# The last product of a gated feed-forward layer: one f32 product per block becomes three float32r products of exactly split operands

## The reference, cut to what matters

```python
def act_qdq(x):                      # 16 bit: one scale over the whole tensor
    qmax = 2.0 ** 15 - 1.0
    scale = jnp.maximum(jnp.max(jnp.abs(x)) / qmax, 1e-12)
    return jnp.clip(jnp.round(x / scale), -qmax - 1.0, qmax) * scale

x = act_qdq(x)
up = act_qdq(x @ lpbq_dequant(w_up).T)        # (8, 512, 768)
gate = act_qdq(x @ lpbq_dequant(w_gate).T)
sig = fixed_qdq_u16(jax.nn.sigmoid(gate))
gate = act_qdq(gate * sig)
o = act_qdq(gate * up)                        # (8, 512, 768)
return o @ lpbq_dequant(w_down).T             # (8, 512, 256), added to x
```

## Time and profile before

| | |
|---|---|
| median of 3 runs | 1388.59 us (1387.4 to 1388.69) |
| span of the profiled execution, first to last instruction | 1382.0 us |
| TensorE (PE) busy | 1284.0 us, 93% |
| VectorE (DVE) busy | 977.2 us, 71% |
| ScalarE (ACT) busy | 839.3 us, 61% |
| GpSimd (POOL) busy | 502.6 us, 36% |
| last block, first product to last | 1295.57 to 1378.6 us |

### The profile page before, as it was taken

How to read it: one execution, slowest core, us unless ns; L and a number is a source line. 1 busy time by engine, 2 the same in 40 slices (tenths; PEclk the granted TensorE clock), 3 DMA queues, 4 the chain that set the end, 5 groups by cost and what they waited for, 6 DMA issues and landing times. The chain is left out here.

```text
span 1382.0 us, 21094 instructions
## 1 busy us (share of the span) xinstructions
PE 1284.0 (93%) x7272; PEld 635.7 (46%) x7272; DVE 977.2 (71%) x1703; ACT 839.3 (61%) x1453; POOL 502.6 (36%) x670
## 2 busy tenths in 40 slices
PE   9999799999999999999999999999998999950799
PEld 5566323334343343434545554555444444420587
DVE  5876598887878878786666788887743435987522
ACT  4455337776777767777565556556553437959432
POOL 4455200235344454434673433333330003639200
PEclk9999869999999999999999999999999999975899
DMA  8999674233424243342343643333110001316132
GB/s 288 376 339 325 230 176 111 82 87 93 124 68 127 78 122 105 93 124 75 99 133 94 197 121 101 93 99 109 33 32 16 1 0 73 155 70 250 57 95 91
DMA packets 88190, 170.74 MB, mean 124 GB/s; under 512 B 14867, under 2 KB 49431, under 8 KB 86551
## 3 DMA queue, kind: packets, MB, share of 16 engines
q1 hardware_dynamic: 87547, 168.16, 39.2%
q10 hardware_dynamic: 539, 1.26, 0.4%
HBM read 108.26 MB, written 60.31 MB: 122 GB/s over the span
## 5 line engine op out<-in xcount | busy, mean ns | idle before, releaser
L1329 DVE TENSOR_REDUCE b_neg_max<-b_score 128x1 f32<-128x512 f32 (+3 forms) x864 | 541.2, 663 | 177.6 <-PE b_score L877 93.5
L1102 ACT ACTIVATE b_probs<-b_exp 128x512 f32<-128x512 f32 (+1 forms) x864 | 463.3, 581 | 281.9 <-PE b_exp L901 281.0
L874 PE MATMUL b_score<-b_k_stack,b_q_stack 97*128 97x512 bf16 (+3 forms) x1024 | 356.2, 351 | 14.7 <-issue 8.8
L901 PE MATMUL b_exp<-b_q_stack,b_k_stack 100*128 100x512 bf16 (+3 forms) x1024 | 344.6, 342 | 6.4 <-ACT b_probs L1102 5.6
L922 PE MATMUL b_av<-b_probs,b_values 128*17 128x512 f32 (+3 forms) x2048 | 228.5, 518 | 3.7 <-POOL b_probs L1200 3.4
L874 PEld LDWEIGHTS b_score<-b_k_stack,b_q_stack 97*128 97x128 bf16 x1024 | 99.8, 98 | 250.7 <-DVE b_neg_max L1329 128.5
L901 PEld LDWEIGHTS b_exp<-b_q_stack,b_k_stack 100*128 100x128 bf16 x1024 | 100.1, 98 | 82.6 <-ACT b_probs L1102 24.9
L1200 POOL TENSOR_SCALAR_AFFINE_SELECT b_probs<-b_probs 128x512 f32<-128x512 f32 x96 | 61.7, 643 | 176.7 <-ACT b_probs L1102 176.2
L1208 POOL CAST b_max_parts<-b_neg_max 128x16 bf16<-128x16 f32 x64 | 12.9, 202 | 286.3 <-DVE b_neg_max L1329 284.1
L877 PE MATMUL b_score<-diag_qk,minus_big 128*128 128x128 bf16 x512 | 112.6, 220 | 0.0
L1756 POOL TENSOR_TENSOR f_hidden<-f_tmp,f_hidden 128x2048 int32<-128x2048 int32 x8 | 44.3, 5532 | 137.7 <-DVE f_tmp L1708 137.7
(11 more groups left out here) (212 smaller groups left out, 1821.4 us busy)
## 6 DMA issues: line engine op xcount, KB each, us to landing
b_q_stack<-s_q SPq DMA_DIRECT2D x384, 64.0 KB
s_k<-a_part_k SPq DMA_DIRECT2D x48, 256.0 KB, 3.3
b_k_stack<-s_k SPq DMA_DIRECT2D x61, 192.0 KB
s_up<-f_up SPq DMA_DIRECT2D x6, 1536.0 KB, 5.0
s_va<-a_va SPq DMA_DIRECT2D x16, 544.0 KB, 5.4
b_values<-s_va SPq DMA_DIRECT2D x16, 544.0 KB, 4.1
a_mask_q<-mask_in SPq DMA_DIRECT2D x8, 1024.0 KB, 8.2
b_k_stack<-s_k SPq DMA_DIRECT2D x61, 128.0 KB
```

Source lines behind the costliest of these rows:

```text
L874: mm = pe.matmul(o, q, KS[half][0:R_MAX, h, 0:w], start=True, stop=causal or not general)
L901: mm = pe.matmul(o, k, QS[half][0:NSTACK, h, q0:T], start=True, stop=not masked)
L1102: nc.scalar.activation(probs[kc][:, h0:h0 + m, q0:T], exp_bank[n % RINGS][:, 0:m * w].rearrange("p (h n) -> p h n", h=m), ACT.Exp).then_in ...
L1329: nc.vector.tensor_reduce(neg_max[u][:, qt, h0:h0 + m], score_bank[n % RINGS][:, 0:m * w].rearrange("p (h n) -> p h n", h=m), AX.X, ALU.ma ...
```

## The change

The product of an f32 tile with f32 weights is replaced by three products in float32r (F32R below), a 4-byte type that keeps fewer bits of the mantissa and that TensorE takes in one pass. `w_downT` is split once into `down_high` (its value rounded to float32r) and `down_low` (what is left, written over `w_downT`). The activation is kept as the rounded integer, without its scale, and split in the same way into `o_high` and `o_low`. TensorE adds low x high, high x low and high x high into the same PSUM bank, 18 products for each row tile where there were 6, and the scale is applied in the last addition.

- POOL makes `down_high` (a copy) and `down_low` (a subtraction), each 128x1536, at the head of its stream in the first block; DVE gets a `memset` of `minus_magic` at the head of its stream there.
- ScalarE: after the two shifts of a half it also makes `o_high` (128x1536, bias -MAGIC), but for batch 0.
- DVE: `unshift` goes; `low` makes `o_low` = (od - MAGIC) - o_high, 128x1536, from two SBUF tiles; for the four pieces of batch 0 it also makes `o_high`. `add` becomes a `scalar_tensor_tensor` (PSUM times scale plus x). The order is low(b, u), add(b-1, u).
- TensorE: 576 products for 192; it waits for `lows`, and for `down_split` once.
- The loops of the third block are unrolled on every engine.
- `o_high` lies in the room of the two `up` tiles, `o_low` in that of `normed`'s batches 2 and on.

```diff
+                    nc.vector.memset(minus_magic[:, :], -MAGIC)
                     nc.vector.memset(sig_unit[:, :], 2.0 ** -16).then_inc(unit_set, 1)
...
+                    nc.gpsimd.tensor_copy(down_high[:, :, :], w_downT[:, :, :]).then_inc(down_split, 1)
+                    pool.wait_ge(down_split, 1)
+                    nc.gpsimd.tensor_tensor(down_low[:, :, :], w_downT[:, :, :], down_high[:, :, :].bitcast(F32), ALU.subtract).then_inc(down_split, 1)
                     for b in range(NB):
                         gates(b)
...
+                    def round_off(b, u):
+                        here = part_of(b, u)
+                        if b > 1 and u == 0:
+                            act.wait_ge(lows, piece(b - 2, pieces(b - 2) - 1))
+                        shift(od[b % 2][:, 0:MINE, here], at(b)[:, 0:MINE, here], "prod")
+                        shift(od[b % 2][:, MINE:FC, here], whole(b)[:, MINE:FC, here], "prod").then_inc(shifted, 1)
+
+                    def high(b, u):
+                        here = part_of(b, u)
+                        act.wait_ge(shifted, piece(b, u))
+                        if b > 1:
+                            act.wait_ge(full, 2 * (b - 2) + u + 1)
+                        nc.scalar.activation(o_high[b % 2][:, :, here], od[b % 2][:, :, here], ACT.Identity, bias=minus_magic[:, 0:1]).then_inc(highs, 1)
+
+                    for b in range(NB):
+                        for u in range(pieces(b)):
+                            round_off(b, u)
+                            if b > 0:
+                                high(b, u)
...
                                 t = 2 * u + j
-                                if pieces(b) == TT:
-                                    pe.wait_ge(dequant, t + 1)
-                                for f in range(FC):
-                                    mm = pe.matmul(down[2 * half + u][:, j, :], od[half][:, f, t * P:(t + 1) * P], w_downT[:, f, :], start=(f == 0), stop=(f == FC - 1))
+                                if b == 0:
+                                    pe.wait_ge(lows, piece(0, t))
+                                terms = [(o, wt, f) for o, wt in ((o_low, down_high), (o_high, down_low), (o_high, down_high)) for f in range(FC)]
+                                for n, (o, wt, f) in enumerate(terms):
+                                    mm = pe.matmul(down[2 * half + u][:, j, :], o[half][:, f, t * P:(t + 1) * P], wt[:, f, :], start=(n == 0), stop=(n == len(terms) - 1))
                             mm.then_inc(full, 1)
...
-                            unshift(od[half][:, :, here], od[half][:, :, here], "prod").then_inc(dequant, 1)
+                    def low(b, u):
+                        here = part_of(b, u)
+                        if b == 0:
+                            dve.wait_ge(shifted, u + 1)
+                            nc.vector.tensor_scalar(o_high[0][:, :, here], od[0][:, :, here], -MAGIC, None, ALU.add).then_inc(first_highs, 1)
+                            dve.wait_ge(first_highs, u + 1)
+                        else:
+                            dve.wait_ge(highs, 2 * (b - 1) + u + 1)
+                        if b > 1:
+                            dve.wait_ge(full, 2 * (b - 2) + u + 1)
+                        nc.vector.scalar_tensor_tensor(out=o_low[b % 2][:, :, here], in0=od[b % 2][:, :, here], scalar=-MAGIC,
+                                                       in1=o_high[b % 2][:, :, here].bitcast(F32), op0=ALU.add, op1=ALU.subtract).then_inc(lows, 1)
...
-                            nc.vector.tensor_tensor(x, down[2 * half + u][:, :, :], x, ALU.add).then_inc(added, 1)
+                        nc.vector.scalar_tensor_tensor(out=x, in0=down[2 * half + u][:, :, :], scalar=scales["prod"][0][:, 0:1], in1=x,
+                                                       op0=ALU.mult, op1=ALU.add).then_inc(added, 1)
```

More of the change, by code:

```diff
@@ L9 @@
 F32 = mybir.dt.float32
+F32R = mybir.dt.float32r
 BF16 = mybir.dt.bfloat16
@@ L1470, in gated_ffn_phase @@
         hidden = sb("hidden", [P, FC, NB, T], F32)
+        down_high, down_low = sb("down_high", [P, FC, D], F32R), weights.down_low
+        o_high = [nc.alloc_sbuf_tensor_at(f"f_o_high{i}", [P, FC, T], F32R, offset=nc.sbuf_base + 4 * FC * T * i) for i in range(2)]
+        o_low = [nc.alloc_sbuf_tensor_at(f"f_o_low{i}", [P, FC, T], F32R, offset=const["normed_at"] + 4 * (2 * TT * D + FC * T * i)) for i in range(2)]
+        down_split = sem("down_split")
         up = [sb(f"up{i}", [P, FC, T], F32) for i in range(2)]
@@ L1478, in gated_ffn_phase @@
         units = {"act": sig_unit, "prod": sb("unit_prod", [P, 1], F32)}
+        minus_magic = sb("minus_magic", [P, 1], F32)
+        first_highs = sem("first_highs")
         unit_set = sem("unit_set")
@@ L1834, in gated_ffn_phase, with piece, part_of @@
             x_stored = [sem(f"x_stored{i}") for i in range(2)]
-            shifted, dequant, full, added = (sem(f"down_{n}") for n in ("shifted", "dequant", "full", "added"))
-            EXTRA = TT - 2
+            shifted, highs, lows, full, added = (sem(f"down_{n}") for n in ("shifted", "highs", "lows", "full", "added"))
             def pieces(b):
-                return TT if known(b) and b == 0 else 2
+                return TT if b == 0 else 2
+            def piece(b, u):
+                return u + 1 if b == 0 else TT + 2 * (b - 1) + u + 1
+            def part_of(b, u):
+                n = T // pieces(b)
+                return slice(u * n, (u + 1) * n)
             with nc.Block() as block:
@@ L1847, in rows @@
                         return dram["out"][b].rearrange("(t p) d -> p t d", p=P)
-                    def step(b, half, k):
-                        if not known(b):
-                            wait_apart(sp, x_stored[half], 16 * k)
+                    for b in range(NB):
+                        half = b % 2
+                        if b > 1:
+                            sp.wait_ge(x_stored[half], 16 * (b // 2))
                         sp.dma_start(XL[half], rows(b)).then_inc(x_landed[half], 16)
-                        if not (known(b) and b == 0):
-                            wait_apart(sp, added, 2 * b)
+                        if b > 0:
+                            sp.wait_ge(added, 2 * b)
                             sp.dma_start(rows(b - 1), XL[1 - half]).then_inc(x_stored[1 - half], 16)
-                    over_batches(sp, step)
                     for u in range(2):
@@ L1865, in _ @@
                 def _(act):
[L1866 to L1875, removed]
+                    def round_off(b, u):
[10 more added lines that the diff above has]
+                        nc.scalar.activation(o_high[b % 2][:, :, here], od[b % 2][:, :, here], ACT.Identity, bias=minus_magic[:, 0:1]).then_inc(highs, 1)
+                    for b in range(NB):
+                        for u in range(pieces(b)):
+                            round_off(b, u)
+                            if b > 0:
+                                high(b, u)
                 @block.tensor
                 def _(pe):
-                    def step(b, half, k):
+                    keep_busy(pe, const, over[1], 11)
+                    pe.wait_ge(down_split, 2)
+                    for b in range(NB):
+                        half = b % 2
                         for u in range(2):
-                            if pieces(b) == 2:
-                                pe.wait_ge(dequant, 2 * b + u + 1 + EXTRA)
-                            if not known(b):
+                            if b > 0:
+                                pe.wait_ge(lows, piece(b, u))
+                            if b > 1:
                                 pe.wait_ge(added, 2 * (b - 2) + u + 1)
@@ L1891, in step @@
+                                for n, (o, wt, f) in enumerate(terms):
+                                    mm = pe.matmul(down[2 * half + u][:, j, :], o[half][:, f, t * P:(t + 1) * P], wt[:, f, :], start=(n == 0), stop=(n == len(terms) - 1))
                             mm.then_inc(full, 1)
-                    keep_busy(pe, const, over[1], 11)
-                    over_batches(pe, step)
                 @block.vector
                 def _(dve):
[L1898 to L1902, removed]
-                            unshift(od[half][:, :, here], od[half][:, :, here], "prod").then_inc(dequant, 1)
@@ L1917, in _ @@
-                    over_batches(dve, step)
-                    add(NB - 1, 1, NB // 2 - 1)
+                    def low(b, u):
[6 more added lines that the diff above has]
+                            dve.wait_ge(highs, 2 * (b - 1) + u + 1)
+                        if b > 1:
+                            dve.wait_ge(full, 2 * (b - 2) + u + 1)
+                        nc.vector.scalar_tensor_tensor(out=o_low[b % 2][:, :, here], in0=od[b % 2][:, :, here], scalar=-MAGIC,
+                                                       in1=o_high[b % 2][:, :, here].bitcast(F32), op0=ALU.add, op1=ALU.subtract).then_inc(lows, 1)
@@ new lines, in add @@
```

(16 more changed lines are left out.)

1 line of the change is left out of this document (added).

## The result

| | before | changed |
|---|---|---|
| median of the runs | 1387.99 us (1383.9 to 1388.69, 4 runs) | 1376.91 us (1372.42 to 1378.31, 4 runs) |
| ratio | | 0.9918, 95% interval 0.9897 to 0.9939 |
| span of the profiled execution | 1382.0 us | 1376.6 us |

The change made the kernel 11.1 us faster (interval about 8.5 to 14.3). The forecast was a saving of 17.2 us, to 1371.4 us; the measured time lies inside the stated range of 1368.8 to 1378.5, 5.5 us above that value.

What follows compares the result with a forecast made beforehand. TensorE's products were taken to bound the third block (busy 83.11 of 83.20 us). Against the span of 1382.0: -20.1 +1.06 +0.05 +1.7 +0.06 = -17.2, so 1364.8, plus 6.6 around it 1371.4 us; range 1368.8 to 1378.5.

Steps and rivals of the forecast that it cites:

- third rival: Third block: another engine or a half-hidden load sets the pace; 1374 to 1384 us, chance 0.13.
- One pass in place of four: Third block, TensorE: 576 float32r products of one pass replace 384 instructions of f32 products; 20.1 us saved.
- rival of 0.216 us a product: Third block: a float32r product streams like every other 4-byte operand, at 0.216 us; 1433 us, chance 0.10.
- The size of the product's term: Third block: products 0.109 us apart, 62.95 us in all where 83.04 stood; 20.1 us saved.
- bf16 row: Profile row of four bf16 products of the same 256 columns, 0.110 us each, used as a lower bound for float32r's price.
- The load: Third block, TensorE: loads of the stationary tile near 140 ns, of which about 57 ns grows with the columns.
- That a load hides at all: Third block: loads hide under products in flight; the rival, an exposed load, gave 0.166 us a product, 1404 us, chance 0.03.
- DVE behind POOL: Head of first block: DVE's first unshift waits for POOL's subtraction, gates 1.7 us later; rival of no hold-up 1369.6, chance 0.12.
- The first product: Start of third block: DVE's high, a wait and low replace unshift, so the first product starts 1.06 us later.
- ScalarE, DVE and the transfers hidden: Third block, per batch: ScalarE 7.2 us and DVE 5.1 under TensorE's 7.85; transfers 7.2 against 11.8 us.
- margin of 0.3 us a half: Third block: ScalarE's spare time under TensorE's products in each half of a batch, 0.3 us.
- low end: Lower limit of the stated range: no stall at the head, 1369.6, and products 108 ns apart, 1368.8 us.

Runs made afterwards that it cites:

- bf16 run: The changed kernel with GpSimd's split of the weights moved later and all four split tiles in bfloat16 instead of float32r: 1367.03 us, ratio 0.9861 to the kernel before.
- split_later: The changed kernel with GpSimd's copy and subtraction waiting until DVE has made its last unshift of x: 1371.56 us, ratio 0.9900.

## Why the prediction was right in sign and too large in size

The number lies inside the stated range, and partly by width: the forecast gave its own sum 1369 to 1374 with a chance of 0.62, and 1376.9 lies in the range of its third rival (1374 to 1384, chance 0.13), of which the stated range took in the lower half. Of the 6.2 us between the saving that was forecast (17.2) and the one in the traces (11.0), 5.8 are the pace of the products, 0.9 the head, and 0.4 at the first product go the other way.

- **One pass in place of four** held. 576 instructions and one load each. The rival of 0.216 us a product is refuted.
- **The size of the product's term failed.** The step "a pass that stands alone is a quarter of 432 ns, or 108" took the f32 stream for four passes at bf16's pace. Measured: 119 ns, 68.7 us for 62.95, 5.8 us less gain. The bf16 run shows the pace that was forecast, in the same loop, so the price is the type's. The bf16 row had been the right price for bf16 alone.
- **The load** was forecast near 140 ns, like the transpose's. It is 188 ns, the f32 half-product's. The third rival had named that case ("a float32r load that grows like the f32 half's, 107 ns, has no room under 109 and could make the pace 0.12"), and its pace is what came. Its mechanism is half of the cause at most, by the estimate above: the load costs some 4 ns of the 10, and the rest goes with the columns streamed.
- **That a load hides at all** held: 188 ns beside products 119 apart, and 98 beside 109 in the bf16 run. The rule of the Trainium skill (TensorE: Matmul & The Clock Gate, Part 3), that a load overlaps products in flight only when they use other rows of the array, is contradicted by both; the same part also speaks of a background weight buffer into which a load can go ahead, and the traces fit that.
- **DVE behind POOL** held in mechanism and in size. Forecast +1.7, measured +1.6 where the transposes ran at full clock; split_later undoes it, and it was made again in the kernel before. The Trainium skill (SBUF — State Buffer, Who interferes with whom) has it as a rule: the two share a pair of ports, and of a DVE instruction in a two-port mode and a POOL one, the one that starts first holds the pair for its whole length and the other waits. The traces agree with the wait: 2616 ns against 744; in which mode the DVE instruction ran they do not show. What was missed is 1.1 us of half clock under the first transposes. Every later profile shows such a stretch within some microseconds of that place and the profiled execution of before does not; whether the change makes it likelier was not settled, since the kernel before was profiled once, though with the split put in it has the stretch. DVE's stall is not what brings it, at least not alone, since split_later has the stretch and no stall.
- **The first product**: forecast +1.06, measured +0.64. High (0.56) and low (0.96) came out at 1.52 where 1.63 was said, and the first product followed low after 0.14 us, where it followed the unshift of the earlier trace rows after 0.42 (1295.15 to 1295.57). The forecast took `unshift` for what released it; it was the 11 products of constants, and some 0.3 us of the longer way to low were hidden behind them. That gain was not in the sum.
- **ScalarE, DVE and the transfers hidden** held, with more room than said; no addition of the changed kernel's last block waited for a transfer. ScalarE's half is 3.46 us (1308.22 to 1311.68 in the changed kernel, high 1.58 us long), TensorE's became 36 x 0.119 = 4.3, and high waits for `full` (3.2 us in 4 waits). The margin of 0.3 us a half is 0.8. DVE's low takes 1.75 us (1.81 forecast).
- **The sum again**: -14.3 (products) +0.64 (first product) +0.06 (last addition, 0.75 for 0.69) +2.64 (head) = -11.0 us; the spans from the first reduction give -11.0, the medians -11.1. The `memset`, 0.06 in the forecast, lies ahead of that reduction and moved it by 0.02. One sum of the forecast is off: its low end, no stall and 108 ns, comes to 1369.1 and not 1368.8.
- **The time around the span**, taken as 6.6 us, is 1.7 in the changed kernel (1378.31 to 1376.6). Every other profiled run lies 1.7 to 1.8 us above its span, so the profiled execution of before was likely its fastest, 1383.9. Since only the difference went into the forecast, it cost nothing; the profiled pair alone (5.4 us) would have misled. And the runs of the kernel before do not lie 1.3 us apart, as three of them did: 17 of them reach from 1383.49 to 1390.32.

## What to carry to other kernels

Price an operand type by a row of that type, or keep its pace as an open term: three products in float32r cost 3 x 119 ns and not 3/4 of one in f32 (432 ns), and that difference took 5.8 of the 20.1 us expected of the products. Before giving an idle engine work, look at what its neighbours do at that moment: five microseconds of POOL, needed 240 us later, held up the one DVE instruction on the path, and one wait moved it away at no cost elsewhere. And ask of a released instruction what its own engine was still doing: here the first product had stood behind filler products, not behind DVE. When products are made cheaper, compute the next engine's period at once, since here it lay only 1.7 us a batch below TensorE's (6.9 against 72 x 0.119 = 8.6).

## What the runs showed of the hardware that was not expected

- A float32r product of 128 stationary and 256 moving columns costs 119 ns in a row of them, bf16 109, f32 432 (two instructions). With 512 moving columns 233 against 216.
- A float32r load is about as long as an f32 half's, 188 ns for 190 (134 with 64 columns). Products of 128 moving columns with full loads are still 112 to 113 ns apart; that the load sets this floor is likely, not shown.
- An f32 tensor_scalar of DVE in SBUF that starts under a tensor_tensor of POOL waits for its end: 2609 to 2655 ns for 744, in eight profiles.
- Single stretches of 3.4 us at half clock (granted clock 0.50) come and go from one execution to the next of the same kernel; one in the projections or at the end of attention went with 1.55 to 1.7 us lost each time, and one under the first transposes of the gated layer with 1.1.
